# Moving the lead-in of a second feed-forward stage into the last unit of an attention stage, and re-ordering the first group of the first one

## Chip, cores and metric

The kernel runs on one core of one Trainium2 chip. It is one program that is launched once. The metric is its device time in microseconds (us), the median of several runs; the profile is of one further execution. Instruction lines (L1046 and so on) are those of the kernel before; where a line of the changed kernel is meant, the text says so.

## What is computed

The input is x of shape (2, 4096, 256). The reference is a layer of three residual blocks; the first and the third use the same weights:

```python
    x = L0_attn_x
    x = x + 0.5 * _L0_ffn_ref(_layernorm(x, axis=-1), L0_ffn_Wr, L0_ffn_We)
    x = x + _L0_attn_ref(_layernorm(x, axis=-1), L0_attn_Wq, L0_attn_bq, L0_attn_Wk, L0_attn_bk, L0_attn_Wv, L0_attn_bv, L0_attn_Wo, L0_attn_bo)
    x = x + 0.5 * _L0_ffn_ref(_layernorm(x, axis=-1), L0_ffn_Wr, L0_ffn_We)
```

The feed-forward block sends each token to the 2 best of 8 experts (a 256 x 256 matrix each), with a capacity per expert that is counted in the order of the tokens. The attention has 16 heads of 16 features, rotary positions and a softmax over 4096 keys, and ends in an output projection with bias.

## The kernel before

The program is three blocks of code, one after the other; all five engines meet at a barrier between two of them.

**First block (front_phase).** It takes the 8192 tokens in 16 groups of 512: layer norm, routing, experts, and the projections of q, k, v of the groups before. Ahead of the loop each engine does the routing of group 0. TensorE (PE) turns and projects it (`turn`, `router`), waits until the low parts of all weights are made (`pe.wait_ge(s_wl, 2)`), and then does `positions(0)`. VectorE (DVE) makes these low parts, `wel` (L667), `wql` (L671) and `wvl` (L672), and then the choice of experts `pick(0)`. GpSimd (POOL) makes the low part of the activations (`lower`, L765) and the counts (`route`, L786 to L791).

**Attention (attend_phase).** It works on 64 units: 16 pairs of heads times 4 stretches of 1024 queries. A unit has 32 steps over the keys (j = 0 to 31); a step has two halves, and in each half PE does two score products (L1036, 512 columns, operands on 50 of 128 rows), in their shadow two products for the row maxima of the next unit (L1015, on the other rows), and then the products of four earlier exponentials with v (L1046, `times_v`; recorded as 8 rows). ScalarE (ACT) takes the exponential of each score tile (L1114, 128 a unit); DVE takes the maxima (L1139). Three banks hold scores: `score` waits for the exponential three tiles back. The last unit has no maxima to make: `find` returns at once, so DVE has nothing to do in it.

SyncE (SP) runs the transfers in the order of the code. In the last pair of heads it fetches, behind unit 60, what the third block needs first (`fetch`), and behind unit 62 it writes the reciprocals of the softmax sums and reads them back for the first two groups (`fetch_reciprocals`, L1245 and L1248). Ahead of this it must send the output of unit 62 (L964), which ACT copies after tile 8 of unit 63 (`take_output`, L1105).

**Third block (back_phase).** Again 16 groups of 512 tokens. The lead-in of group 0 runs before the loop: bias product (L1429), `spread_out` (L1372, lays the reciprocals over the rows), `normalise_heads` (L1510), `project` (L1379), `add_residual` (L1517), `statistics`, root (ACT, L1464), `newton`, `normalise` (ACT, L1471), `turn` (L1389), `turned` (ACT, L1479 and L1481), `router` (L1398), `pick`, `route`, `positions` (L1405, L1406), and for group 1 everything up to `add_residual`. Then come the expert products of group 0 (L1422) in chunks of 6 matmuls and the weighted sums on DVE (L1559).

## Time and profile before

| | us |
|---|---|
| median of 3 runs (6259.62 to 6266.20) | 6264.52 |
| the profiled execution, its own time | 6264.74 |
| its span in the trace | 6262.9 |

| stretch of the profiled execution | from | to |
|---|---|---|
| first block | 0 | about 670 |
| attention | about 674 | 5757.7 |
| lead-in of the third block | 5757.7 | 5791.4 |
| expert loop of the third block | 5791.4 | 6262.9 |

Busy shares over the span are PE 99%, DVE 94%, ACT 78%, POOL 6%. PE's ends are modelled, so its share says little; the timelines say more. In a timeline a row is a run of like instructions: start, time from the first start to the last end, engine, line, operation, output and inputs, count, and in brackets the idle time ahead of it and what ended it. Granted clock 1.00 is 2.4 GHz, 0.50 is 1.2 GHz.

### The profile page before, as it was taken

How to read it: one execution, taken by the hardware profiler on the slowest of the kernel's cores; microseconds unless marked ns; L12 is line 12 of the kernel's file. 1: busy time of each engine (PE TensorE's matmuls, PEld its weight loads, DVE VectorE, ACT ScalarE, POOL GpSimd, SP SyncE). 2: the span in 40 equal slices, each digit the busy share in tenths (PEclk: the TensorE clock that was granted, in tenths of full speed). 3: DMA queues.
4: the chain of work that ended last, by engine and by line, in shares of the span. 5: the costliest groups of instructions: out<-in, count | busy, mean ns of one | idle time of the engine just before them, and what ended most of it. 6: DMA issues, size and time to landing. Idle time of an engine off the chain costs nothing. (4 is left out here: it accounts for less than half of the span.)

```text
span 6262.9 us, 158275 instructions
## 1 busy us (share of the span) xinstructions
PE 6191.1 (99%) x54276; PEld 2765.9 (44%) x54276; DVE 5907.4 (94%) x6787; ACT 4864.3 (78%) x8953; POOL 398.4 (6%) x604
## 2 busy tenths in 40 slices
PE   8999999999999999999999999999999999999999
PEld 6887333333333333333333333333333333333787
DVE  7998999999999999999999999999999999992777
ACT  4443488888888888888888888888888888887221
POOL 3443100000000000000000000000000000000222
PEclk9998799999999999999999999999999999999999
DMA  2335010101010101010101010101010101000110
GB/s 84 124 121 145 12 17 14 17 14 17 14 17 14 17 14 17 14 17 14 17 14 17 14 17 14 17 14 17 14 17 14 17 14 17 3 22 23 56 56 31
DMA packets 121413, 175.91 MB, mean 28 GB/s; under 512 B 62016, under 2 KB 78944, under 8 KB 117728
## 3 DMA queue, kind: packets, MB, share of 16 engines
q1 hardware_dynamic: 120928, 168.25, 11.8%
q8 instruction: 451, 7.39, 0.5%
q14 instruction: 34, 0.28, 0.0%
HBM read 98.47 MB, written 69.73 MB: 27 GB/s over the span
## 5 line engine op out<-in xcount | busy, mean ns | idle before, releaser
L1139 DVE TENSOR_REDUCE at_mx<-at_m 128x1 f32<-128x1024 f32 x4028 | 4928.7, 1224 | 49.9 <-PE at_m L1015 29.4
L1114 ACT ACTIVATE at_ex<-at_s 128x512 f32<-128x512 f32 x8192 | 4450.1, 595 | 608.1 <-PE at_s L1036 39.4
L1036 PE MATMUL at_s<-at_q,at_k 50*128 50x512 f32 x8192 | 2997.4, 444 | 0.0
L1015 PE MATMUL at_m<-at_k,at_q 48*128 48x512 f32 x8040 | 2928.9, 443 | 2.7 <-issue 2.7
L1046 PE MATMUL at_po<-at_ex,at_v 128*32 128x256 f32 x32816 | 2625.0, 392 | 0.0
L1015 PEld LDWEIGHTS at_m<-at_k,at_q 48*128 48x128 f32 x8040 | 1185.2, 185 | 1662.7 <-DVE at_mx L1139 1592.9
L1046 PEld LDWEIGHTS at_po<-at_ex,at_v 128*32 128x32 f32 x32816 | 646.4, 108 | 1488.8 <-issue 751.2
L1036 PEld LDWEIGHTS at_s<-at_q,at_k 50*128 50x128 f32 x8192 | 1212.0, 185 | 41.0 <-ACT at_ex L1114 40.6
L986 POOL COPY at_v<-at_vst 128x1024 f32<-128x1024 f32 x16 | 16.6, 1036 | 4457.4 <-DMA at_vst<-v_by_head 4457.2
L1422 PE MATMUL bk_ps<-sh_weh,bk_xl 128*128 128x512 f32 x512 | 169.4, 412 | 6.2 <-DVE bk_acc L1559 6.2
L1464 ACT ACTIVATE bk_root<-bk_var 128x4 f32<-128x4 f32 x16 | 3.3, 205 | 212.8 <-DVE bk_var L1531 212.8
L1422 PE MATMUL bk_ps<-sh_wel,bk_xh 128*128 128x512 f32 x512 | 161.3, 396 | 0.0
L1422 PE MATMUL bk_ps<-sh_weh,bk_xh 128*128 128x512 f32 x512 | 161.3, 396 | 0.0
L1559 DVE SCALAR_TENSOR_TENSOR bk_acb<-bk_ps,bk_weight,bk_acc 128x256 f32<-128x256 f32 x192 | 92.8, 484 | 55.4 <-PE bk_ps L1422 46.4
L1559 DVE SCALAR_TENSOR_TENSOR bk_acc<-bk_ps,bk_weight,bk_acb 128x256 f32<-128x256 f32 x256 | 123.9, 484 | 9.1
L373 PE MATMUL fr_ps<-sh_weh,fr_xl 128*128 128x512 f32 x352 | 115.4, 409 | 5.2 <-DVE fr_acc L598 4.9
L510 ACT ACTIVATE fr_parts<-fr_rot 128x1024 fp32r<-128x1024 f32 x32 | 34.2, 1069 | 105.8 <-DVE fr_rot L653 105.8
L373 PE MATMUL fr_ps<-sh_weh,fr_xh 128*128 128x512 f32 x352 | 111.5, 398 | 0.0
L373 PE MATMUL fr_ps<-sh_wel,fr_xh 128*128 128x512 f32 x352 | 111.2, 397 | 0.0
L1422 PEld LDWEIGHTS bk_ps<-sh_wel,bk_xh 128*128 128x128 f32 x512 | 96.6, 189 | 23.1
L1422 PEld LDWEIGHTS bk_ps<-sh_weh,bk_xh 128*128 128x128 f32 x512 | 96.5, 188 | 23.4
L1422 PEld LDWEIGHTS bk_ps<-sh_weh,bk_xl 128*128 128x128 f32 x512 | 91.4, 189 | 31.9 <-DVE bk_acc L1559 10.7
(195 smaller groups left out, 2913.5 us busy)
## 6 DMA issues: line engine op xcount, KB each, us to landing
at_q<-q_parts SPq DMA_DIRECT2D x96, 256.0 KB, 4.9
at_k<-k_parts SPq DMA_DIRECT2D x96, 256.0 KB, 6.2
q_parts<-fr_parts SPq DMA_DIRECT2D x64, 256.0 KB, 2.2
k_parts<-fr_parts SPq DMA_DIRECT2D x64, 256.0 KB, 2.5
attended<-at_o SPq DMA_DIRECT2D x256, 34.0 KB
fr_x<-in_x SPq DMA_DIRECT2D x16, 512.0 KB, 4.3
after_ffn<-fr_acc SPq DMA_DIRECT2D x16, 512.0 KB, 3.0
v_by_head<-fr_v SPq DMA_DIRECT2D x16, 512.0 KB, 4.4
```

Of the source, the lines that this page charges most:

```text
L373: last = pe.matmul(pe_s[BANK[n]][:, :], (xh, xl)[a][0][u][:, c, i * P:(i + 1) * P], (weh, wel)[b][:, c, EP * k:EP * (k + 1), :].rearrange( ...
L510: ac.activation(pt[:, 0, w, :, :], rot[:, :, :], ACT.Copy).then_inc(s_hi, 1)
L986: gp.tensor_copy(V[p][:, :, :, 0:HD], vst[p][:, :, :, :]).then_inc(s_vh, 1)
L1015: ins = pe.matmul(pm[w][:, h * QB:(h + 1) * QB], Q[p][rows, base + i * P:base + (i + 1) * P], K[p][rows, c * CW + h * QB:c * CW + (h + 1) ...
L1036: pe.matmul(ps[event(t) % NS], K[p][rows, j * P:(j + 1) * P], Q[p][rows, sb_ * QU + g * QB:sb_ * QU + (g + 1) * QB], start=True, stop=True ...
L1046: last = pe.matmul(po[W * t:W * (t + 1), cols], V[p][:, w, j, :], Ex[QUAD * (j % NX) + t][:, cols], start=start and half == 0, stop=stop a ...
L1114: ac.activation(Ex[QUAD * (j % NX) + 2 * g + 1 - half][:, :], ps[event(t) % NS], ACT.Exp)\
L1139: ve.tensor_reduce(out=mx[u][:, i, c:c + 1], in_=first[(k + 2) % len(first)][:, 0:CW] if opens else pm[w][:, :], op=ALU.max, axis=AX.X)\
L1422: last = pe.matmul(pe_s[BANK[n]][:, :], (xh, xl)[a][u][:, c, i * P:(i + 1) * P], (weh, wel)[b][:, c, EP * k:EP * (k + 1), :].rearrange("p ...
L1464: ac.activation(root[:, :], var[:, :], ACT.Sqrt).then_inc(s_root, 1)
L1559: ve.scalar_tensor_tensor(out=dst, in0=pe_s[BANK[i * NP + e // EP]][:, (e % EP) * D:(e % EP + 1) * D], scalar=weight[u][:, i, e:e + 1], in ...
```

## The change

It has four parts.

1. The lead-in of the third block moves into unit 63 of the attention. PE's part is cut in 26 pieces, set between steps of the unit. The rows that ACT handled (normalising, turning) are done by DVE; the root is done by GpSimd as a power of 0.5. Only the exponential of the routing stays on ACT, ahead of its step 29. The banks of the row maxima (`at_m`) serve as room.
2. SP's fetches for groups 2 and 3 move from the third block behind the read of the reciprocals in the attention.
3. ACT's loop over the units is cut at step 10 of a unit in place of its start; the order of the scores is that of all other units (`PAIRED` is KT, so the other order is never taken).
4. In the first block PE does the first two expert chunks ahead of `positions(0)` and waits there for `wel` alone; DVE makes `wql` and `wvl` in group 0, between its chunks 12 and 13.

```diff
@@ first block, PE, ahead of the loop
-                pe.wait_ge(s_wl, 2)
+                pe.wait_ge(s_wl, 1)
+                experts(0, 0, 0, 2)
                 positions(0)
...
@@ first block, DVE, body (taken away: the same three lines ahead of pick(0))
                     if here:
                         combine(g, u, it, 10, 13)
+                    if isinstance(g, int) and g == 0:
+                        ve.wait_ge(s_wh, 2)
+                        ve.tensor_tensor(wql[:, :, :, :], pq_in[:, :, :, :], wqh[:, :, :, :].bitcast(F32), ALU.subtract)
+                        ve.tensor_tensor(wvl[:, :, :], pv_in[:, :, :], wvh[:, :, :].bitcast(F32), ALU.subtract).then_inc(s_wl, 1)
                     if after:
                         pick(g + 1)
...
@@ attention, SP
                         if not more and sb_ == SB - 1:
-                            fetch_reciprocals(sp)
+                            fetch_reciprocals_ahead(sp, ahead, sources, late.s_tick)
+                            for g in range(2):
+                                fetch_group(sp, ahead, late, sources, g + 2, g)
...
@@ attention, PE, last unit
                 pairs(pe, pair)
+                last_unit(0, 2)
+                pe.wait_ge(s_mr, 2 + NPAIR * SB * RED)
+                pe.wait_ge(ahead.s_c, 4 * DMA)
+                for c in range(NC):
+                    last = pe.matmul(pm[0][:, GT:GT + D], ahead.bv[:, c, :], ahead.wo[:, c, :], start=(c == 0), stop=(c == NC - 1))
+                last.then_inc(late.s_bv, 1)
+                last_unit(2, 4)
+                step.spread_out(pe, 0, 0, 0)
+                last_unit(4, 6)
+                pe.wait_ge(late.s_bo, 1)
+                for m in range(TG * NC):
+                    step.project(pe, 0, m, m + 1)
+                    last_unit(6 + m, 7 + m)
+                last_unit(14, 15)
+                step.spread_out(pe, 1, 1, 0)
+                last_unit(15, 18)
+                for c in range(NC):
+                    step.turn(pe, 0, c, c + 1)
+                    last_unit(18 + c, 19 + c)
+                for m in range(2):
+                    step.project(pe, 1, m, m + 1)
+                    last_unit(20 + m, 21 + m)
+                for i in range(TG):
+                    step.router(pe, 0, i, i + 1)
+                    last_unit(22 + i, 23 + i)
+                for m in range(2, TG * NC):
+                    step.project(pe, 1, m, m + 1)
+                    last_unit(24 + m, 25 + m)
+                step.positions(pe, 0)
...
@@ attention, ACT
-                with loop(nc, ac, 0, NPAIR * SB) as u:
-                    unit(u)
+                unit(0, 0, CUT * QUAD)
+                with loop(nc, ac, 0, LAST) as u:
+                    unit(u, CUT * QUAD)
+                    unit(u + 1, 0, CUT * QUAD)
+                unit(LAST, CUT * QUAD, 29 * QUAD)
+                step.exponential(ac, 0)
+                unit(LAST, 29 * QUAD)
...
@@ attention, DVE, behind the maxima
                 invert_sums(ve, ahead, 0)
+                ve.wait_ge(s_s, LAST * TILES + 2)
+                ve.wait_ge(late.s_bv, 1)
+                ve.tensor_tensor(ahead.bo[:, :], ahead.bo[:, :], pm[0][:, GT:GT + D], ALU.add).then_inc(late.s_bo, 1)
+                step.normalise_heads(ve, 0, 0, 0)
+                for j in range(2):
+                    step.add_residual(ve, 0, 0, j)
+                step.statistics(ve, 0, late.y[0])
+                step.newton(ve, 0)
+                step.normalise_here(ve, 0, late.y[0])
+                step.normalise_heads(ve, 1, 1, 0)
+                step.turned_here(ve, 0, 0)
+                step.pick(ve, 0)
+                step.odds(ve, 0)
+                for j in range(2):
+                    step.add_residual(ve, 1, 1, j)
+                step.room(ve, 0)
...
@@ attention, GpSimd, behind its pairs
+                step.biased(gp, 0, 0, 0)
+                step.root_by_power(gp, 0)
+                step.biased(gp, 1, 1, 0)
+                step.lower(gp, 0, 0)
+                step.route(gp, 0, 0)
...
@@ new functions
+def fetch_group(sp, t, late, sources, g, u):
+
+    attended, residual, reciprocals, _, _ = sources
+    hold(sp, late.s_an, g - 1, late.s_tick)
+    for c in range(NC):
+        sp.dma_start(t.at[u][:, c, :], attended(g, c)).then_inc(t.s_at[u], DMA)
+    sp.dma_start(t.rec[u][:, :].bitcast(F32), reciprocals(g)).then_inc(t.s_rec[u], DMA)
+    hold(sp, late.s_xb, g - 1, late.s_tick)
+    sp.dma_start(t.x[u][:, :, :], residual(g)).then_inc(t.s_x[u], DMA)
...
+    def spread_out(pe, n, u, it):
+
+        pe.wait_ge(s_rec[u], it * DMA + DMA)
+        need(pe, s_y, n * 2 - 1)
+        pe.matmul(py[0][:, :], spread[:, :], rec[u][:, :], start=True, stop=True).then_inc(s_pr, 1)
...
+    def root_by_power(gp, n):
+        hold(gp, s_var, n + 1, s_tick)
+        gp.tensor_tensor(root[:, :], var[:, :], r0[:, :], ALU.pow).then_inc(s_root, 1)
+
+    def normalise_here(ve, n, src):
+        ve.wait_ge(s_nw, (n + 1) * NEWTON)
+        for i in range(TG):
+            last = ve.tensor_scalar(xn[:, i, :], src[:, i, :], mv[:, i, 0:1], rs[:, i:i + 1], ALU.subtract, ALU.mult)
+        last.then_inc(s_xn, 1)
+
+    def turned_here(ve, n, u):
+        ve.wait_ge(s_tr, n + 1)
+        for c in range(NC):
+            ve.tensor_copy(xt[:, c, :], pT[c][:, :])
+        for c in range(NC):
+            last = ve.tensor_copy(xh[u][:, c, :], pT[c][:, :])
+        last.then_inc(s_ev, 1)
```

The instructions of PE at the boundary between attention and third block, before. `at_po` is the output of the attention, `bk_py`, `bk_pT` and `bk_pz` are banks of the third block, and "waits" names what the instruction waits for:

```order
L1046 MATMUL at_po<-at_ex,at_v 32x256 x7
L917 UNCONDITIONAL_BRANCH
L1366 UNCONDITIONAL_BRANCH [waits barrier_Pool_Activation_PE_DVE_SP_release]
L1429 MATMUL bk_py<-bk_wo,bk_bv 128x256 [waits bk_const]
L1429 MATMUL bk_py<-bk_wo,bk_bv 128x256
L1372 MATMUL bk_py<-bk_rec,bk_spread 128x512 [waits bk_rec0,bk_recs]
L1379 MATMUL bk_py<-bk_wo,bk_an 128x256 [waits bk_an,bk_bias]
L1379 MATMUL bk_py<-bk_wo,bk_an 128x256 x7
L1389 MATMUL bk_pT<-sh_ident,bk_xn 128x128 [waits bk_xn]
```

The same place now (the lines are those of the changed kernel):

```order
L1438 MATMUL at_m<-bk_chosen,sh_before 128x32 [waits bk_chosen]
L1439 MATMUL at_m<-bk_pre,sh_ones 128x32
L1073 MATMUL at_po<-at_ex,at_v 32x256 [waits at_exp]
L1073 MATMUL at_po<-at_ex,at_v 32x256 x7
L927 UNCONDITIONAL_BRANCH
L1685 UNCONDITIONAL_BRANCH [waits barrier_Pool_Activation_PE_DVE_SP_release]
L1700 MATMUL bk_ps<-sh_weh,bk_xl 128x512 [waits bk_xlow]
L1700 MATMUL bk_ps<-sh_weh,bk_xl 128x512
```

Behind the barrier the expert products come at once; what stood between is ahead of it.

PE in steps 3 to 5 of the last unit, before (`at_s` is a score bank):

```order
L1036 MATMUL at_s<-at_q,at_k 128x512 [waits at_exp] x2
L1046 MATMUL at_po<-at_ex,at_v 32x256 x4
L1036 MATMUL at_s<-at_q,at_k 128x512 [waits at_exp] x2
L1046 MATMUL at_po<-at_ex,at_v 32x256 [waits at_exp]
L1046 MATMUL at_po<-at_ex,at_v 32x256 x3
```

And now, the same steps, with the wait for the reciprocals of group 0 (`bk_rec0`) ahead of step 4:

```order
L1063 MATMUL at_s<-at_q,at_k 128x512 [waits at_exp] x2
L1073 MATMUL at_po<-at_ex,at_v 32x256 x4
L1401 MATMUL at_m<-bk_rec,bk_spread 128x512 [waits bk_rec0]
L1063 MATMUL at_s<-at_q,at_k 128x512 [waits at_exp] x2
L1073 MATMUL at_po<-at_ex,at_v 32x256 [waits at_exp]
L1073 MATMUL at_po<-at_ex,at_v 32x256 x3
```

A product of the lead-in, with a wait of its own, stands in the row of the unit's products.

SP in the last pair, now:

```order
L976 DMA attended<-at_o 17x512 [waits at_mq,at_exp]
L976 DMA attended<-at_o 17x512 x3
L1329 DMA reciprocals<-bk_split 16x512 [waits bk_recs]
L1329 DMA reciprocals<-bk_split 16x512 x15
L1332 DMA bk_rec<-reciprocals 32x512 [waits bk_recout]
L1332 DMA bk_rec<-reciprocals 32x512
L1345 DMA bk_at<-attended 128x512 [waits bk_an]
```

Up to the read of `bk_rec` this order is that of before; the fetch of group 2 behind it is new here.

## Rows read from the trace of the kernel before

**Rows 1.** Timeline of PE at the end of the attention and in the lead-in.

```profile
5754.66 0.73 PE L1036 MATMUL at_s<-at_q,at_k 50*128 50x512 f32 x2
5755.32 2.37 PE L1046 MATMUL at_po<-at_ex,at_v 128*32 128x256 f32 x40
5761.47 1.10 PE L1429 MATMUL bk_py<-bk_wo,bk_bv 128*128 128x256 f32 x4 [3.78 <-PEq L917]
...
5778.00 1.97 PE L1389 MATMUL bk_pT<-sh_ident,bk_xn 128*128 128x128 f32 x8 [7.24 <-ACT bk_xn L1471]
```

**Rows 2.** Chain that ended last, in order of time, same place: start, us, what.

```profile
5785.70 5.68 PE bk_py L1379 x16
5791.43 5.70 PE bk_ps L1422 x24
```

**Rows 3.** Timelines of PE and ACT in the last unit.

```profile
5687.02 0.73 PE L1036 MATMUL at_s<-at_q,at_k 50*128 50x512 f32 x2
...
5700.54 0.73 PE L1036 MATMUL at_s<-at_q,at_k 50*128 50x512 f32 x2
...
5701.08 1.09 ACT L1114 ACTIVATE at_ex<-at_s 128x512 f32<-128x512 f32 x2
```

**Rows 4.** Timelines of PE and ACT in unit 0, at the low clock.

```profile
690.15 0.79 PE L1036 MATMUL at_s<-at_q,at_k 50*128 50x512 f32 x1
...
690.99 1.08 ACT L1114 ACTIVATE at_ex<-at_s 128x512 f32<-128x512 f32 x2 [1.07 <-PE at_s L1036]
...
692.31 0.79 PE L1036 MATMUL at_s<-at_q,at_k 50*128 50x512 f32 x1
```

**Rows 5.** Timeline of SP in the last unit.

```profile
5684.52 8.04 SPq L1245 DMA_DIRECT2D reciprocals<-bk_split  x16
5694.14 0.79 SPq L1248 DMA_DIRECT2D bk_rec<-reciprocals  x2
```

**Rows 6.** The view of line L1248, from issue to landing.

```profile
DMA to landing us min/median/max: 1.9/1.9/1.9
```

**Rows 7.** Chain that ended last, third block; its first row follows an idle PE.

```profile
5820.59 6.01 PE bk_ps L1422 x18
...
5832.34 0.43 PE bk_py L1372
...
5838.57 0.87 PE bk_pT L1389 x8
...
5842.25 1.68 PE bk_pz L1398 x16
5843.94 3.56 PE bk_py L1379 x16
```

**Rows 8.** Stretches: length, busy (count) of PE, PEld, DVE, ACT, POOL, clock, DMA.

```profile
620.00:668.00 48.00, 46.95 (x84) 20.65 (x84) 48.00 (x44) 0.00 (x0) 0.00 (x0) 0.50 0.08 27
688.00:706.00 18.00, 18.00 (x104) 6.07 (x100) 10.12 (x9) 9.28 (x17) 1.97 (x1) 0.50 0.03 7
...
5690.00:5756.00 66.00, 66.00 (x544) 24.33 (x547) 0.00 (x0) 58.33 (x108) 0.00 (x0) 1.00 0.03 7
...
5816.00:5820.00 4.00, 0.46 (x2) 0.03 (x1) 3.93 (x4) 0.23 (x1) 0.43 (x3) 1.00 0.00 0
...
5822.00:5824.00 2.00, 2.00 (x6) 1.58 (x5) 0.96 (x3) 0.00 (x0) 0.00 (x0) 0.50 0.00 0
5824.00:5826.00 2.00, 2.00 (x10) 1.60 (x10) 1.50 (x6) 0.00 (x0) 0.64 (x3) 1.00 0.04 8
```

**Rows 9.** Timelines of PE and DVE in the first group.

```profile
28.50 0.18 PE L356 MATMUL fr_ps2z<-fr_chosen,sh_before 128*128 128x32 bf16 x1 [7.87 <-POOL fr_run L791]
...
19.42 3.37 DVE L671 TENSOR_TENSOR fr_wql<-fr_xn,fr_wqh 128x1024 fp32r<-128x1024 f32 x1
22.72 0.68 DVE L672 TENSOR_TENSOR fr_wvl<-fr_even,fr_wvh 128x512 fp32r<-128x512 f32 x1
...
31.59 0.49 DVE L598 SCALAR_TENSOR_TENSOR fr_acb<-fr_ps,fr_weight,fr_x 128x256 f32<-128x256 f32 x1 [2.65 <-PE fr_ps L373]
```

More of the change, by code:

```diff
@@ L992, in _, with pair @@
                     gp.wait_ge(s_one, 3 + w)
-                def step(r, k, n, more):
+                def pair(r, k, n, more):
                     if more:
@@ L1105, in take_output, with unit @@
                     ac.activation(O[:, :], po[:, :], ACT.Copy).then_inc(s_e, 1)
-                def unit(u):
-                    for t in range(TILES):
+                def unit(u, start=0, end=TILES):
+                    for t in range(start, end):
                         j, half, g = t // QUAD, t % QUAD // 2, t % 2
+                        slot = 2 * half + 1 - g if isinstance(u, int) and u == LAST and j >= PAIRED else 2 * g + 1 - half
                         if t % QUAD == 0:
@@ L1254, in back_phase @@
+def back_phase(nc, name, shared, ahead, late, sources, attended_out, out):
+    _, _, _, sums_of, recs_of = sources
     EP = 2
@@ L1425, in experts @@
                         last.then_inc(s_mm, 1)
-                pe.wait_ge(s_c, 4 * DMA)
-                for c in range(NC):
-                    last = pe.matmul(py[1][:, 0:D], bv[:, c, :], wo[:, c, :], start=(c == 0), stop=(c == NC - 1))
-                last.then_inc(s_bv, 1)
-                pe.wait_ge(s_all, 4)
-                spread_out(0, 0, 0)
-                pe.wait_ge(s_bo, 1)
-                project(0)
-                turn(0)
-                spread_out(1, 1, 0)
-                router(0)
-                project(1)
-                positions(0)
                 def body(g, u, it):
```

560 lines of the change are left out of this document (276 added, 284 removed).

## Prediction, made before the changed kernel had run

> **What bounds the kernel now.** I read the stage borders first, then PE's timeline at the end of the attention. The reader is to see there that PE's last product of the attention ends at 5755.32 + 2.37 = 5757.69, that PE starts again behind the barrier at 5761.47 [rows 1], and that the first expert product comes at 5791.43 [rows 2]. The 29.96 us between are a lead-in in which PE mostly waits; one wait alone is 7.24 us [rows 1]. All of this leaves the place where it stood. The barrier with its 3.78 us stays.
>
> The next question is whether the last unit has room for it. DVE does nothing there for the 66 us that were looked at, and ACT is busy 58.33 of them [rows 8]. But the moved products run on PE. The last unit goes from step 4 at 5687.02 [rows 3] to its last half at 5754.66 [rows 1], 55 halves, so 1.230 us a half. Is that PE's own time or a wait for ACT? The score of 5700.54 has its exponential at 5701.08 [rows 3]: ACT takes a score as soon as it is there, and idles ahead of it. At the low clock the same half takes 692.31 - 690.15 = 2.16 us, with ACT idle for 1.07 of it [rows 4], so there PE surely sets the pace. Cutting these 2.16 us in a part that goes with the clock (0.93 at full clock) and one that doesn't (0.30) gives 1.23 again. I conclude that PE bounds the last unit, and that what is put into it is paid in full.
>
> **The change, part by part.**
>
> (a) Removed: 29.96 us between barrier and first expert product.
>
> (b) The wait at step 4. PE now stands there until the reciprocals of group 0 are read back (`bk_rec0`). SP issues this read at 5694.14 [rows 5]; it lands 1.9 us later [rows 6], at 5696.04. Nothing ahead of it on SP changes: 16 writes take 8.04 us from 5684.52 on [rows 5], behind the output of unit 62, which hangs on the copy behind ACT's tile 8, and that lies ahead of the first inserted piece. PE comes to step 4 at 5687.02 [rows 3], with the bias product ahead of it about 0.9 us later. Behind PE are queued all scores, so ACT stands too. With 0.1 us for the signal and 0.43 us [rows 7] x 2.16/1.23 = 0.76 for the spread product, step 4 begins at 5696.9 and not at 5687.02: +9.9 us, the bias product within it. The bounds are 9.5 (full clock) and 10.5.
>
> (c) The other pieces: group 0 and 1 projected 2 x 3.56, one spread product 0.43, turning 0.87, router 1.68 [rows 7], positions 0.05 (between 5785.70 + 5.68 and 5791.43 [rows 2]): 10.15 us. These rows are runs; now they are 24 short pieces between other shapes. A change of shape costs nothing at best, and at most 0.1 us, a third of the fixed 0.30 of a half with its three groups: 0 to 2.4. I take 0.85, nearer to nothing, since most pieces wait for nothing. +11.0 us. If ACT did bound the unit, these would be free; that is a rival.
>
> (d) The clock. PE is idle for some 8 us at step 4. In the trace an idle PE at 5816 to 5820 is followed by clock 0.50 [rows 8]; so step 4 begins at 1.2 GHz. How long does it stay? In dense expert products it was back within about 3.5 us (18 products from 5820.59, clock 1.00 from 5824 [rows 7, 8]). In the very mix of the attention, unit 0, it was still 0.50 over all of 688 to 706, with PE recorded busy all the time; and in products of maxima alone over 620 to 668 [rows 8]. The nearest row is that of the mix: some 18 us, or 9 halves of 0.93 = 8.4 us, and 0.7 for two or three pieces in them (16 take 5.68 at the low clock [rows 2] against 3.56 [rows 7], 0.27 for a piece of two). +9.1 us. The ends are 1.5 us (dense rows) and the rest of the unit, 56 halves x 0.93 = 52 us and the pieces at 1.8 times their time, 8 us: 60 us.
>
> The Trainium skill, page "TensorE: Matmul & The Clock Gate", section "Part 1: The HAM clock gate (the 'warmup' mystery)", says that the array is slow by default and that sustained activity gives it full clock at the first busy look. By that rule the mix would be back as fast as dense products. The row of unit 0 speaks against it.
>
> (e) The chain behind each piece. PE waited 7.24 us for sum, statistics, root and rows [rows 1]; now five steps, 12.3 us, lie between the last piece of `project(0)` and `turn`. The root on GpSimd and a DVE that copies four tiles of 128 x 512 aren't in the trace; a weighted sum of 128 x 256 takes DVE 0.49 [rows 9], so the copies some 4 us, against three steps (7.4 us) up to the router. From router to the first expert product it was 5.7 us [rows 2]; the exponential now stands 9.8 us behind it. Nothing, then; if the root took over 4 us, PE would stand for the excess. SP's new transfers for groups 2 and 3 stand behind the reciprocals and ahead of the last output, some 25 steps early: nothing. ACT's loop has the same body: nothing.
>
> (f) The first expert products now follow an idle of 3.78 us. Such a start costs 6.01 us for 18 products [rows 7] against 18/24 x 5.70 = 4.28 [rows 2]: +1.7 us (0 to 3).
>
> (g) First group. PE idles 7.87 us ahead of `positions` [rows 9]; two expert chunks fill part of it. `pick` comes up to 3.37 + 0.68 = 4.05 us earlier, and with it the first weighted sum, at 31.59 before [rows 9]. Then DVE does the two subtractions at group 0's end. They took 4.05; by the 0.68 of the smaller one, which has half the elements, the two would take 2.0 where nothing slows them, and a part falls into DVE's idle time. I take 2.0 back: -2.0 us, between -4.05 and 0, for no more is given back than was won.
>
> **Sum.** -29.96 + 9.9 + 11.0 + 9.1 + 1.7 - 2.0 = -0.3 us. The profiled execution took 6264.74 by its own clock, 0.2 above the median of 6264.52. So 6264.
>
> **The rivals.**
>
> 1. The clock is back quickly (18 in 100). For it: pieces are dense full-array products, and in dense rows it took 3.5 us. Against it: unit 0, and the first two steps have no pieces. Then (d) is 1.5: 6264 - 7.6 = 6256.5. The same time follows from the skill's rule above.
> 2. The clock doesn't come back in the last unit (12 in 100). This is the one that ends slower: without maxima the scores use 50 of 128 rows, and products of maxima alone never got the clock back in 48 us [rows 8]. Against it: at full clock the same unit holds it [rows 8], and the pieces add dense work. Then (d) is 60: 6315. It decides from 45 us at the low clock on; if it comes back between 25 and 60 us (9 in 100), 6267 to 6284.
> 3. ACT bounds the unit, the pieces are hidden (8 in 100). For it: ACT is busy 58.33 of 66 us [rows 8]. Against it: exponentials start at the arrival of their scores [rows 3]. Then (c) is 0: 6253, and with a quick clock 6245.
> 4. The wait at step 4 isn't there, since the reciprocals come earlier than rows 5 say (3 in 100): without (d) and without (b) but for 1.3 of pieces, 6246.
>
> **How the numbers follow.** The forecast, a net of nothing, has 50 in 100, with its own range 6255 to 6274. The range for 8 in 10 takes in rivals 1 and 3 but for the latter's end, and the late return of the clock: 6250 to 6288. A measurement of this kernel can tell some 0.2%, 12.5 us, from no change. Faster by more: most of rivals 3 and 4 and a little of 1 and the forecast, 0.13. Slower by more: rival 2, the late half of its neighbour and an unforeseen stall, 0.21. Within: 0.66.
>
> **What would show each step.** In the profile after: PE idle by some 8 us ahead of `spread_out` with the DMA `bk_rec` as releaser (b); granted clock 0.50 behind it, and where it returns (d); halves of 1.23 us without a piece and about 1.70 with one (c), or 1.23 for both (rival 3); the first expert product some 3.8 us behind the last product of the attention (a), the first four microseconds of them slow (f); DVE's first weighted sum at about 27.5 us (g). The prediction is wrong if the clock behaves otherwise than in unit 0, or if a piece costs much more than its row.

## The result and the profile after

The changed kernel takes 6317.88 us (median of 4 runs, 6305.74 to 6323.36) against 6262.07 us before (4 runs beside it, 6259.52 to 6266.20). The ratio is 1.0083, 95% interval 1.0071 to 1.0095: slower by 0.8%; the two medians are 55.8 us apart. The forecast was 6264 us with a range up to 6288. The second of the rivals is what came, "the clock doesn't come back in the last unit", at 6315 us.

The profiled execution took 6322.34 us, its span is 6320.5. The first view to open is the timeline of PE around step 4 of the last unit; it answers to rows 3. Lines are those of the changed kernel: L1063 scores, L1073 weighted values, L1401 the spread product, L1409 a piece of the projection, L1430 one of the router, L1700 expert products. In a row of PE, `50*128 50x512` means that 50 rows and 128 columns of the array hold the fixed operand and 512 columns stream through it. A router piece is two products in the code and stands as x4: the trace has two records for each product of it.

```profile
5688.93 0.73 PE L1063 MATMUL at_s<-at_q,at_k 50*128 50x512 f32 x2
5689.59 0.64 PE L1073 MATMUL at_po<-at_ex,at_v 128*32 128x256 f32 x8
5698.18 0.79 PE L1401 MATMUL at_m<-bk_rec,bk_spread 32*128 32x512 f32 x1 [7.96 <-DMA bk_rec<-reciprocals]
5698.90 1.22 PE L1063 MATMUL at_s<-at_q,at_k 50*128 50x512 f32 x2
...
5707.54 1.22 PE L1409 MATMUL at_m<-bk_wo,bk_an 128*128 128x256 f32 x2
5708.70 1.22 PE L1063 MATMUL at_s<-at_q,at_k 50*128 50x512 f32 x2
...
5713.02 1.22 PE L1409 MATMUL at_m<-bk_wo,bk_an 128*128 128x256 f32 x2
...
5791.01 1.02 PE L1430 MATMUL at_m<-sh_wr,bk_xt 128*128 128x8 f32 x4
5791.96 1.22 PE L1063 MATMUL at_s<-at_q,at_k 50*128 50x512 f32 x2
```

Ahead of the wait a pair of scores takes 0.73 us, behind it 1.22. That is the low clock, and it is still there at 5791.96. The second view is the table of stretches: length, then busy time and count of PE, PEld, DVE, ACT and POOL, then the granted clock, DMA share and GB/s.

```profile
5692.00:5700.00 8.00, 1.82 (x3) 0.78 (x3) 0.92 (x2) 0.27 (x1) 0.00 (x0) 0.55 0.19 48
5700.00:5720.00 20.00, 20.00 (x86) 6.96 (x86) 0.37 (x1) 8.41 (x16) 0.00 (x0) 0.50 0.17 57
...
5780.00:5800.00 20.00, 20.00 (x88) 8.26 (x84) 0.00 (x0) 7.60 (x14) 0.87 (x1) 0.50 0.00 1
...
5830.00:5848.00 18.00, 18.00 (x94) 6.39 (x97) 1.48 (x3) 6.51 (x12) 0.21 (x1) 0.50 0.00 0
...
5856.00:5860.00 4.00, 4.00 (x16) 2.81 (x16) 2.96 (x12) 0.10 (x1) 0.00 (x0) 0.93 0.11 37
```

The clock is 0.50 (1.2 GHz) in every stretch from 5700 to 5848 us, with PE recorded busy all the time, and comes back only among the expert products. It stays low although a piece that uses all rows and columns of the array, 1.16 us of work, stands between the scores every 5.48 us (5707.54, 5713.02). The same unit stood at 1.00 over 66 us before [rows 8]. The third view is PE's timeline at the end of the attention, which answers to rows 1 and 2.

```profile
5845.11 3.64 PE L1073 MATMUL at_po<-at_ex,at_v 128*32 128x256 f32 x32
5851.38 1.19 PE L1700 MATMUL bk_ps<-sh_weh,bk_xl 128*128 128x512 f32 x2 [2.63 <-PEq L927]
...
5856.61 0.63 PE L1700 MATMUL bk_ps<-sh_weh,bk_xl 128*128 128x512 f32 x2
...
5868.46 0.73 PE L1700 MATMUL bk_ps<-sh_weh,bk_xl 128*128 128x512 f32 x2 [0.56 <-DVE bk_acc L1749]
...
5881.50 0.73 PE L1700 MATMUL bk_ps<-sh_weh,bk_xl 128*128 128x512 f32 x2 [2.02 <-DVE bk_acc L1749]
```

The lead-in is gone as meant: only the barrier, 2.63 us without work of PE, lies between the last product of the attention and the first of the experts.

The span grew by 57.6 us, and the timelines of both kernels give all of it:

| part | before | after | us |
|---|---|---|---|
| start of the last unit (ACT's copy in its step 2) | 5682.11 | 5684.46 | +2.35 |
| from there to the first score of step 4 | 4.91 | 14.44 | +9.53 |
| from there to the end of the attention (5757.69, 5848.75) | 70.67 | 149.85 | +79.18 |
| from there to the first expert product (5791.43, 5851.38) | 33.74 | 2.63 | -31.11 |
| from there to the end | 471.47 | 469.12 | -2.35 |

The row of +79.18 is what has to be explained. The forecast had 11.0 + 9.1 there. The first row, +2.35, can't be put down to the change: see (g) below.

### The profile page after: what moved, and what is told of

Read it like the earlier page. It is cut to its first block and busy times, and to the rows that moved or that the text cites. A ratio compares the mean times of both kernels' runs of the same rounds, so it can differ in the third digit from the quotient of the medians.

```text
span 6320.5 us, 158147 instructions
## 1 busy us (share of the span) xinstructions
PE 6253.8 (99%) x54276; PEld 2780.1 (44%) x54276; DVE 5911.3 (94%) x6795; ACT 4856.8 (77%) x8942; POOL 400.1 (6%) x606
## 5 line engine op out<-in xcount | busy, mean ns | idle before, releaser
L1063 PE MATMUL at_s<-at_q,at_k 50*128 50x512 f32 x8192 | 3025.0, 448 | 0.0
L1073 PE MATMUL at_po<-at_ex,at_v 128*32 128x256 f32 x32816 | 2651.6, 395 | 0.0
L1073 PEld LDWEIGHTS at_po<-at_ex,at_v 128*32 128x32 f32 x32816 | 649.1, 108 | 1506.1 <-issue 779.7
L1063 PEld LDWEIGHTS at_s<-at_q,at_k 50*128 50x128 f32 x8192 | 1223.7, 186 | 55.6 <-ACT at_ex L1177 42.9
L1700 PE MATMUL bk_ps<-sh_weh,bk_xl 128*128 128x512 f32 x512 | 169.7, 413 | 7.2 <-DVE bk_acc L1749 4.4
L1700 PE MATMUL bk_ps<-sh_wel,bk_xh 128*128 128x512 f32 x512 | 160.7, 395 | 0.0
L1700 PE MATMUL bk_ps<-sh_weh,bk_xh 128*128 128x512 f32 x512 | 160.6, 395 | 0.0
L1700 PEld LDWEIGHTS bk_ps<-sh_wel,bk_xh 128*128 128x128 f32 x512 | 96.7, 189 | 22.4
L1700 PEld LDWEIGHTS bk_ps<-sh_weh,bk_xh 128*128 128x128 f32 x512 | 96.7, 189 | 22.3
L1700 PEld LDWEIGHTS bk_ps<-sh_weh,bk_xl 128*128 128x128 f32 x512 | 91.1, 189 | 34.9 <-DVE bk_acc L1749 11.8
```

Source lines behind the costliest of these rows:

```text
L1063: pe.matmul(ps[event(t) % NS], K[p][rows, j * P:(j + 1) * P], Q[p][rows, sb_ * QU + g * QB:sb_ * QU + (g + 1) * QB], start=True, stop=True ...
L1073: last = pe.matmul(po[W * t:W * (t + 1), cols], V[p][:, w, j, :], Ex[QUAD * (j % NX) + t][:, cols], start=start and half == 0, stop=stop a ...
L1700: last = pe.matmul(pe_s[BANK[n]][:, :], (xh, xl)[a][u][:, c, i * P:(i + 1) * P], (weh, wel)[b][:, c, EP * k:EP * (k + 1), :].rearrange("p ...
```

## The experiments

The theory after this reading (A): PE's idle time at step 4 takes the clock down, and the last unit's own products can't bring it back. The rivals: the small pieces hold the clock down with or without the wait (B), or they are what keeps it from coming back (C).

**e1, the reciprocals early.** SP stores and fetches them in the last unit but one:

```
-                        if not more and sb_ == SB - 1:
+                        if not more and sb_ == SB - 2:
                             fetch_reciprocals_ahead(sp, ahead, sources, late.s_tick)
+                        if not more and sb_ == SB - 1:
                             for g in range(2):
                                 fetch_group(sp, ahead, late, sources, g + 2, g)
```

> The changed kernel with one thing moved: SyncE stores and fetches the reciprocals of the first two groups during the last unit but one (about 14 us ahead of where they are needed) instead of behind the output of that unit, so that bk_rec0 has landed long before step 4 of the last unit. The pieces stay where they are. Theory A, the 8 us idle of TensorE takes the clock down, and without it the clock stays at 1.00 for the last unit: the profile shows no idle of TensorE at L1401 ahead of step 4, windows of the last unit at 1.00, the unit about 74 us shorter (8 of the wait, about 66 of the low clock, from the changed kernel's 167 us between ScalarE's copy and the first expert product against 82 before + 8 + 11 of pieces), so about 6248 us. Theory B, the small pieces (32- to 256-column float32 products and the change between shapes) hold the clock down with or without the wait: only the 8 us go, the windows stay at 0.50 for more than 100 us, about 6314 us.

Measured: 6249.10 us (6239.07 to 6264.57, 10 runs) against 6264.29 before, ratio 0.9971 (0.9960 to 0.9982). The median is 69 us under that of the changed kernel, as A said and B excludes. But the ten runs fall apart: 6239 to 6242 in four, 6248 to 6265 in six. The profiled one, 6261.25, is of the second kind, and its stretches and PE's timeline (L1064 scores, L1431 router pieces) show why:

```profile
5690.00:5720.00 30.00, 30.00 (x224) 11.45 (x223) 8.59 (x23) 22.24 (x42) 3.79 (x5) 1.00 0.01 2
5734.00:5736.00 2.00, 2.00 (x14) 0.87 (x14) 0.00 (x0) 1.18 (x3) 0.00 (x0) 1.00 0.03 8
5736.00:5738.00 2.00, 2.00 (x15) 1.18 (x14) 0.00 (x0) 0.99 (x2) 0.00 (x0) 0.77 0.00 0
5738.00:5740.00 2.00, 2.00 (x11) 0.70 (x10) 0.00 (x0) 1.09 (x2) 0.00 (x0) 0.50 0.00 0
5740.00:5780.00 40.00, 40.00 (x170) 14.86 (x168) 2.43 (x13) 16.38 (x31) 2.29 (x11) 0.50 0.00 1
```

```profile
5733.61 0.61 PE L1431 MATMUL at_m<-sh_wr,bk_xt 128*128 128x8 f32 x4
5734.15 0.73 PE L1064 MATMUL at_s<-at_q,at_k 50*128 50x512 f32 x2
...
5736.60 0.62 PE L1431 MATMUL at_m<-sh_wr,bk_xt 128*128 128x8 f32 x4
5737.16 1.22 PE L1064 MATMUL at_s<-at_q,at_k 50*128 50x512 f32 x2
```

Step 4 and 50 us behind it run at 1.00, pieces and all. Then the clock falls at 5737.16, right behind the second router piece, with PE never idle, and stays down to the end of the unit. So B is wrong for the whole, and something of it is right at one place.

**e2, the wait alone.** The kernel before, with one line added at step 4 of the last unit, and no piece:

```
+                            if isinstance(u, int) and u == NPAIR * SB - 1 and j == 4 and half == 0:
+                                pe.wait_ge(ahead.s_rec[0], DMA)
```

> The kernel before, with one wait added and nothing else: TensorE waits at step 4 of the last unit for the landing of bk_rec0. No piece is moved. Theory A with its second half, that the last unit's own products (scores and weighted values, no maxima) can't bring the clock back: windows at 0.50 from about 5700 us to the end of the unit, 28 steps at about 2.16 us over the 2.1 they take at the full clock (+60 us) and 8 us of wait, so about 6330 us. Rival C, that it is the pieces between the steps which keep the clock from returning: the clock is back within some 20 us as in unit 0, and the kernel takes 8 + about 9 more than before, about 6280 us.

Measured: 6330.50 us (6322.85 to 6337.03, 4 runs), ratio 1.0102 (1.0083 to 1.0121). One wait on PE costs 66 us. PE's timeline and the stretch behind the wait:

```profile
5687.93 0.64 PE L1046 MATMUL at_po<-at_ex,at_v 128*32 128x256 f32 x8
5697.36 1.22 PE L1036 MATMUL at_s<-at_q,at_k 50*128 50x512 f32 x2 [8.79 <-DMA bk_rec<-reciprocals]
...
5825.51 2.05 PE L1431 MATMUL bk_py<-bk_wo,bk_bv 128*128 128x256 f32 x4 [4.03 <-PEq L917]
```

```profile
5700.00:5815.00 115.00, 115.00 (x532) 37.12 (x531) 0.00 (x0) 57.67 (x107) 0.00 (x0) 0.50 0.00 1
```

0.50 for 115 us and more, without a single piece. From step 4 to the end of the attention (5825.51 - 4.03 = 5821.48) it is 124.12 us, where before it was 70.67: the low clock alone costs 53.4 us, on top of the wait's 8.8. C falls; both halves of A hold.

**e8, the wait and a run of full-array products behind it.** What does the unit lack to bring the clock back? The kernel e2 with 16 products of 128 rows and 256 columns behind the wait:

```
+                                pe.wait_ge(ahead.s_c, 4 * DMA)
+                                pe.wait_ge(s_mr, 2 + NPAIR * SB * RED)
                                 pe.wait_ge(ahead.s_rec[0], DMA)
+                                for n in range(16):
+                                    pe.matmul(pm[n % 2][:, 0:D], ahead.wo[:, 0, 0:P], ahead.wo[:, 1, :], start=True, stop=True)
```

> e2_wait_only (the kernel before with the 8.8 us wait at step 4 of the last unit) and directly behind the wait 16 products of 128 rows and 256 columns in float32 (wo by wo, into the two buffers of the maxima, which nobody reads any more), about 0.85 us each at the low clock and about 0.4 at the full. e2_wait_only stayed at 0.50 from 5697 us to the end of the unit, 6330.5 us. Theory A': what the unit lacks to bring the clock back is products that fill all rows and columns; the burst brings it back within 5 to 9 us and the rest of the unit runs at 1.00: 6330 - 60 + 8, about 6278 us. Rival: once down, the clock stays down for the unit whatever is in between, or falls again at once: about 6330 + 13 = 6343 us.

Measured: 6281.79 us (6277.14 to 6287.48, 7 runs), ratio 1.0030 (1.0019 to 1.0041). 49 us less than e2, though 9.85 us of useless work were added. The two waits ahead are for the weights and the free banks that these products need; the row names the read of the reciprocals as the last to come. PE's timeline (here L1063 is the added product, 16 of them recorded as 32) and the stretches:

```profile
5688.45 9.92 PE L1063 MATMUL at_m<-bk_wo 128*128 128x256 f32 x32 [8.81 <-DMA bk_rec<-reciprocals]
5698.30 0.73 PE L1036 MATMUL at_s<-at_q,at_k 50*128 50x512 f32 x2
```

```profile
5692.00:5694.00 2.00, 2.00 (x6) 1.62 (x5) 0.00 (x0) 0.00 (x0) 0.00 (x0) 0.50 0.00 0
5694.00:5696.00 2.00, 2.00 (x10) 1.72 (x10) 0.00 (x0) 0.00 (x0) 0.00 (x0) 0.98 0.00 0
5700.00:5760.00 60.00, 60.00 (x491) 22.01 (x490) 0.00 (x0) 52.98 (x98) 0.00 (x0) 1.00 0.00 1
```

The clock is back 5.6 us after the burst began (5688.45 to about 5694), and the very unit that couldn't raise it then holds it for 60 us. From its first score behind the burst to the end of the attention it takes 70.68 us, as before. Raising and holding are two things.

**e3 and e4, the first group.** Both put the first group back to the order of before (VectorE's two subtractions ahead of the first `pick`, no expert chunk ahead of `positions`); e3 is otherwise the changed kernel, e4 is e1.

```
-                pe.wait_ge(s_wl, 1)
-                experts(0, 0, 0, 2)
+                pe.wait_ge(s_wl, 2)
                 positions(0)
...
```

> The changed kernel with the first group as in the kernel before (subtractions of the projection's low parts ahead of the first pick, no experts ahead of positions); the last unit as in the changed kernel. What the trace suggests: the changed order wins 5.1 us at the first expert product (23.4 for 28.55 us), loses 2.1 by two waits for bk-style sums and 2.6 + low clock at 54.1 us behind the subtractions that VectorE now does ahead of group 1's pick, and stands 1.9 to 2.4 us behind at the last unit; so this kernel should have ScalarE's copy of the last unit at about 5682.1 instead of 5684.5 us and take about 2 us less, about 6316 us. Rival: the 2.35 us come from elsewhere (chance of the first block's transfers), and the copy stands at 5684.5 here too.

> Both of the former: reciprocals fetched early and the first group as before. Theory A and additive parts: about 6246 us, 2 us under e1_rec_early and 16 under the kernel before; first expert product of the second network at about 5776 us. Theory B: about 6312 us.

Measured: e3 6323.89 us (4 runs, ratio 1.0094, 1.0077 to 1.0111), e4 6244.68 us (6240.01 to 6269.42, 10 runs, ratio 0.9977, 0.9963 to 0.9991). e3's ratio and that of the changed kernel (1.0083, 1.0071 to 1.0095) overlap, so the times can't tell 2 us here. ACT's copy in the last unit is at 5677.53 in e3, neither at the 5682.1 that was expected nor at the rival's 5684.5. In e4 seven runs lie at 6240 to 6245 and three at 6262 to 6269. Its profiled execution is one of the seven, and it is where the pieces can be priced at the full clock (L1058 scores, L1404 projection, L1425 router):

```profile
5685.06 0.50 PE L1396 MATMUL at_m<-bk_rec,bk_spread 32*128 32x512 f32 x1
5685.48 0.73 PE L1058 MATMUL at_s<-at_q,at_k 50*128 50x512 f32 x2
...
5690.40 0.70 PE L1404 MATMUL at_m<-bk_wo,bk_an 128*128 128x256 f32 x2
5691.03 0.73 PE L1058 MATMUL at_s<-at_q,at_k 50*128 50x512 f32 x2
...
5737.63 0.61 PE L1425 MATMUL at_m<-sh_wr,bk_xt 128*128 128x8 f32 x4
5738.17 0.73 PE L1058 MATMUL at_s<-at_q,at_k 50*128 50x512 f32 x2
...
5773.57 0.70 PE L1695 MATMUL bk_ps<-sh_weh,bk_xl 128*128 128x512 f32 x2 [2.62 <-PEq L921]
```

A projection piece moves the next score by 0.63 us, a router piece by 0.54. From the first score of step 4 to the end of the attention (5770.95) it is 85.47 us, 14.80 more than before. The mean of e4's ten runs, on which its ratio rests, is less far below before than the median, because of the three.

**e5, e6, e7, the router pieces.** Theory D says that a stretch whose only pieces are narrow (8 columns) can take the clock; E says that it falls by chance anywhere. E has some support in the kernel before: in the four series that stand beside the experiments, 3 to 5 of its 17 to 30 runs are above 6270 us, at a mean granted clock of 0.986 to 0.988 against 0.988 to 0.991 in the others, with none of the moved work. No trace of such a run exists. e5 puts each router piece beside a projection piece, e6 puts all four in one lump, e7 issues each twice. The base of all is e4. The edit of e5:

```
                 for i in range(TG):
                     step.router(pe, 0, i, i + 1)
+                    step.project(pe, 1, 2 + i, 3 + i)
                     last_unit(22 + i, 23 + i)
-                for m in range(2, TG * NC):
+                last_unit(26, 30)
+                for m in range(6, TG * NC):
                     step.project(pe, 1, m, m + 1)
                     last_unit(24 + m, 25 + m)
```

The edit of e6:

```
-                for i in range(TG):
-                    step.router(pe, 0, i, i + 1)
-                    last_unit(22 + i, 23 + i)
+                step.router(pe, 0)
+                last_unit(22, 26)
```

The edit of e7:

```
                 for i in range(TG):
+                    need(pe, late.s_ev, 1)
+                    for c in range(NC):
+                        pe.matmul(pm[1][:, (TG + i) * E:(TG + i + 1) * E], late.xt[:, c, i * P:(i + 1) * P], shared[1][:, c, :],
+                                  start=(c == 0), stop=(c == NC - 1))
                     step.router(pe, 0, i, i + 1)
```

> e4_both (reciprocals early, first group as before) with the same pieces in another order: each of the four router pieces (four products of 8 columns, 0.61 us) stands in one step with a projection piece of the second group (256 columns, 0.70 us) instead of in a step of its own; steps 26 to 29 have no piece. Three of ten executions of e4_both took 6262 to 6269 us and the other seven 6240 to 6245; in the profiled execution of e1_rec_early the granted clock fell to 0.50 at 5737.2 us, right behind the second router piece, with no idle of TensorE. Theory D, it is the stretch of steps with nothing but narrow pieces that takes the clock: with wide products beside them nearly all executions are at 6240 to 6245 us, mean clock 0.991 or more, median about 6242. Rival E, the last unit's own mix loses the clock by chance wherever the pieces stand: about three in ten still at 6262 to 6269 us.

> e4_both with all four router pieces in one lump of 16 products (about 2.2 us) ahead of step 22, steps 23 to 25 without a piece. Theory D: the stretch with narrow products alone is shorter over all (one lump and three plain steps), yet the densest narrow stretch is longer; if the narrow products themselves take the clock it falls in at least as many executions as in e4_both (3 in 10), at this one place. Rival E: as e4_both, 3 in 10 by chance, median about 6244 us. If what counts is the alternation of narrow pieces with score steps over some 12 us, it falls in fewer, median about 6242.

> e4_both with the suspected cost doubled: each router piece is issued twice (the first time into columns that nobody reads; its values are not used). Adds 4 x about 0.5 = 2 us at the full clock. Theory D: the clock falls in nearly every execution, at about the router pieces, median about 6265 us with mean clock 0.987 to 0.988. Rival E: 2 us on top of e4_both, median about 6247 us, three in ten with a fallen clock.

Measured, with the runs of each in us:

| kernel | median | ratio to before | runs |
|---|---|---|---|
| e4 | 6244.68 | 0.9977 (0.9963 to 0.9991) | 7 at 6240 to 6245, 3 at 6262 to 6269 |
| e5 | 6255.10 | 0.9989 (0.9980 to 0.9998) | 9 at 6249 to 6258, 2 at 6264 and 6265 |
| e6 | 6268.43 | 1.0006 (0.9996 to 1.0015) | all 10 at 6260 to 6279 |
| e7 | 6265.64 | 0.9999 (0.9987 to 1.0011) | 3 at 6244 to 6246, 7 at 6259 to 6276 |

The same work in one lump leaves all ten runs at 6260 and above, where spread over four steps three were. That the clock fell at the lump is seen in the one trace, and for the other nine runs it is read from their times and mean clocks (0.985 to 0.988). The stretches of e6 show the place; the lump is at 5739.35:

```profile
5739.00:5741.00 2.00, 2.00 (x23) 1.66 (x15) 0.00 (x0) 0.74 (x2) 0.00 (x0) 1.00 0.03 8
5741.00:5743.00 2.00, 2.00 (x14) 0.78 (x13) 1.43 (x8) 1.09 (x2) 0.00 (x0) 0.70 0.00 0
5743.00:5750.00 7.00, 7.00 (x31) 2.52 (x32) 0.66 (x4) 3.26 (x6) 1.40 (x7) 0.50 0.00 0
```

D is borne out by e6. e7 points the same way, seven of ten against three of ten, but so few runs can't part the two, and its traced execution kept the clock. e5 missed its number, 6255 for 6242. Its traced execution kept the clock through all router pieces, the last of which ended at about 5748, and lost it some 10 us later, at a place that I hadn't looked at:

```profile
5755.38 0.64 PE L1068 MATMUL at_po<-at_ex,at_v 128*32 128x256 f32 x8
5757.17 0.99 PE L1058 MATMUL at_s<-at_q,at_k 50*128 50x512 f32 x2 [1.16 <-ACT at_ex L1174]
...
5758.97 1.22 PE L1058 MATMUL at_s<-at_q,at_k 50*128 50x512 f32 x2
```

```profile
5756.52 2.56 ACT L1174 ACTIVATE at_ex<-at_s 128x512 f32<-128x512 f32 x5 [1.85 <-issue]
```

PE waits 1.16 us for ACT, and ACT had stood 1.85 us for nothing the trace shows ("issue"). A gap like it is in e4 (1.72 us, which the trace puts down to a score of PE), where projection pieces around it left PE a wait of 0.40 us only. e5's two runs at 6264 and 6265 have no trace; rival E had expected some of that kind.

**e9 and e10, cover.** The projection pieces are laid so that steps 26 to 28 have one too. e9 has the first group of before, e10 the changed one.

```
-                for m in range(2):
-                    step.project(pe, 1, m, m + 1)
-                    last_unit(20 + m, 21 + m)
+                step.project(pe, 1, 0, 1)
+                last_unit(20, 22)
                 for i in range(TG):
                     step.router(pe, 0, i, i + 1)
+                    step.project(pe, 1, 1 + i, 2 + i)
                     last_unit(22 + i, 23 + i)
-                for m in range(2, TG * NC):
+                for m in range(5, TG * NC):
                     step.project(pe, 1, m, m + 1)
-                    last_unit(24 + m, 25 + m)
+                    last_unit(21 + m, 22 + m)
+                last_unit(29, KT)
```

> e5_router_beside with the pieces without a router partner moved: projection pieces of the second group at steps 20, 22 to 25 (beside the router pieces) and 26, 27, 28; steps 21, 29, 30 and 31 have none. In e5_router_beside the clock fell at 5757.2 us in the profiled execution and in most others (9 of 11 at 6252 us or more where a kept clock gives 6240 to 6245), behind steps 26 to 29 without a piece and a wait of 1.16 us for ScalarE's exponential, which itself had stood 1.85 us for no releaser at one place of its straight-line code; in e4_both, with pieces there, the same standstill made TensorE wait only 0.40 us and the clock stayed. Theory D with its second half (narrow pieces, and a wait of a us where the steps have no wide products, each can take the clock): both causes are gone, nearly all executions at 6240 to 6246 us, median 6243, mean clock 0.991 or more. Rival E, chance falls wherever the pieces stand: 3 in 10 at 6255 to 6269 us.

> e9_cover with the first group in the changed kernel's order (first expert pieces ahead of the positions, the projection's low parts subtracted later). If the first group's new order wins what was forecast: 2 us less than e9_cover, about 6241 us median, all executions within 5 us. If it loses what the one profiled execution seemed to show (last unit 2.35 us later than before): 6245 us.

Measured: e9 6246.60 us (6239.91 to 6254.70, 9 runs, ratio 0.9974, 0.9964 to 0.9984), e10 6246.15 us (6239.75 to 6256.06, 9 runs, ratio 0.9973, 0.9964 to 0.9983). No run is above 6256.1 any more; none of 18 is in the group at 6260 and above, which had three of e4's ten. But in each kernel four of nine runs are at 6250 to 6256. PE still waits 0.66 us (e9) and 0.60 us (e10) for ACT there. The two medians are 1.5 to 1.9 us above e4's.

**e11, ACT back in its loop.** e10, with the 88 straight-line exponentials of the last unit back in the loop, and the router's exponential behind them; DVE's `add_residual` of group 1 also moves ahead of `odds`:

```
-                unit(0, 0, CUT * QUAD)
-                with loop(nc, ac, 0, LAST) as u:
-                    unit(u, CUT * QUAD)
-                    unit(u + 1, 0, CUT * QUAD)
-                unit(LAST, CUT * QUAD, 29 * QUAD)
+                with loop(nc, ac, 0, NPAIR * SB) as u:
+                    unit(u)
                 step.exponential(ac, 0)
-                unit(LAST, 29 * QUAD)
...
-                step.odds(ve, 0)
                 for j in range(2):
                     step.add_residual(ve, 1, 1, j)
+                step.odds(ve, 0)
```

> e10_cover_new_group with ScalarE's part of the last unit put back into its loop (no straight-line code of 88 exponentials), the router's exponential of group 0 behind the unit's last exponential instead of at step 29, and VectorE's add_residual of group 1 ahead of odds. In the profiled executions with the straight-line code ScalarE stood 1.7 to 2.0 us with no releaser at about 5754 us and TensorE then waited 0.40 to 1.16 us; four of nine executions of e9_cover and of e10_cover_new_group took 6250 to 6256 instead of 6240 to 6246 us. Theory F, that this small wait still takes the clock in those executions: the standstill and TensorE's wait are gone, all executions at 6238 to 6245, median about 6241 us. Rival: the spread comes from elsewhere (unit 0, the first block), the 6250 to 6256 stay in about four of ten, median 6246, or the later exponential holds up the first weighted sum of the second network by 1 to 2 us.

Measured: 6243.36 us (6239.83 to 6247.33, 5 runs) against 6262.50 before, ratio 0.9964 (0.9951 to 0.9977). PE has no wait in the whole unit, and the stretches stand at 1.00:

```profile
5680.00:5720.00 40.00, 40.00 (x298) 15.13 (x297) 8.38 (x23) 30.11 (x57) 5.95 (x9) 1.00 0.10 32
5720.00:5760.00 40.00, 40.00 (x305) 16.77 (x301) 7.36 (x20) 28.28 (x53) 3.78 (x8) 1.00 0.09 29
```

None of five runs is above 6248, against eight of eighteen in e9 and e10. That fits F, but doesn't show it: five runs are few, no trace of a run at 6250 to 6256 exists, and the rival that the spread comes from elsewhere stands. e12 below has neither the pieces nor the straight-line code, and its runs spread nearly as far, 6254 to 6267 us; unit 0 makes such a spread, see (g). The later exponential cost the first expert product 1.13 us (its wait is 3.75 us for 2.62), and the clock is at 0.50 behind this longer wait (5774 to 5776), so that from there to the end e11 takes 468.24 us for e10's 466.85.

**e12, the first group alone** in the kernel before; the edit is e3's with plus and minus exchanged.

> The kernel before with the changed order of the first group and nothing else. As forecast: 2 us less than before, 6262 for 6264 us. First expert product at about 23 us for 28.5; the transposes that stand at 45.5 us before at about 43. Rival: the 2.6 us wait at 54 us and the low clock behind it eat the gain, no difference or up to 2 us slower.

Measured: 6262.23 us (12 runs) against 6262.50, ratio 0.9995 (0.9986 to 1.0003): too small for the times. The traces can price it at an early mark, the transposes at about 105 us. In the nine traces with the old order (before, e2 to e9) they start at 105.47, 108.63, 108.27, 105.79, 108.85, 108.69, 108.17, 105.81 and 107.24 us, in the five with the new one (after, e1, e10, e11, e12) at 107.83, 103.91, 106.45, 105.17 and 103.86. The means are 107.4 and 105.4: 2.0 us gained, less than the spread within either group.

## Why the prediction was wrong, by its steps

**(d), the clock, is the step that failed.** It took 9.1 us "by the nearest row", unit 0, "the very mix of the attention". Unit 0 isn't the mix of the last unit. Every step of unit 0 also has products of maxima for the unit to come, and the last unit has none; I had written that difference down myself in the second rival, and gave it 12 in 100. Unit 0's clock came back at 690 to 709 us, depending on the trace, so the 18 us weren't a bad reading of unit 0. Scores and weighted values alone left it at 0.50 for the rest of the unit in e2. That it's the missing products of maxima which make this difference is argued and not shown: no kernel had them behind such a wait. The upper end that I had worked out and set aside was near: its 52 us for the halves are 53.4 in e2, and its 60 with the pieces are 79.18 - 14.80 = 64.4 in the changed kernel, at e4's price for the pieces. By the medians e8 saves more, 48.7 us and the burst's 9.85, 58.6 in all; what is beyond 53.4 lies outside this stretch, and where the last unit begins differs by 8.9 us between the two traces alone, see (g). The idle of 4 us at 5816 [rows 8] was rightly read: an idle PE takes the clock down. The rows of dense products [rows 7, 8] were too: e8 needed some 5.6 us. What neither row said is whether *this* work can raise the clock. The range should have had the full remaining time in it, and even 60 us would have put its end at 6315, 3 us short: (c) was too small as well.

The Trainium skill, "TensorE: Matmul & The Clock Gate", section "Part 1: The HAM clock gate (the 'warmup' mystery)", was rightly set aside as a forecast: by its rule sustained activity releases the throttle at the first busy look, and here 150 us of work with PE recorded busy didn't, where e8's unbroken run of products on the full array did. The second half of what that page says, in "HAM oscillation — how this bites in real kernels", that a wait for a DMA between bursts is what throttles PE, agrees with e2 against before (1.00 and 0.50 in the last unit).

**(b), the wait at step 4,** was right: +9.9 forecast, +9.53 measured, and its parts too (7.96 us of idle, the read issued at 5696.30 and landed 1.8 to 2.1 us later). The whole stands 2 us later than forecast, since the unit began later.

**(c), the pieces,** was undersized. 11.0 us were forecast from step 4 on, 14.80 measured at the full clock (e4). A projection piece costs 0.63 and not 3.56 / 8 = 0.445 (16 x 0.185 = 3.0 us), a router piece 0.54 and not 0.42 (0.5), and 0.40 is the wait for ACT. These come on top of the 10.15 of the rows and make 14.1; a turning piece, 0.58 for 0.435, adds 0.3, and 0.4 isn't placed. The bound for a change of shape, "at most 0.1 us", was too low: it is 0.12 to 0.19 for these pieces. At the low clock a projection piece is 1.16 us (5707.54 to 5708.70), a router piece 0.95. So (c) and (d) together at their upper end gave 71 us and measured 79.2. Rival 3, hidden pieces, is excluded by the same rows.

**(a)** was right (33.74 of before became 2.63; the barrier alone is 1.15 shorter). **(e)** was right in all kernels: PE waits for nothing of the chain. The root on GpSimd takes 1.03 us and the four copies on DVE 2.57 (the bound was 4). What wasn't seen is ACT's standstill in its new straight-line code, under "same body: nothing". **(f)** the slow first products are there, from 5851.38 to about 5856.6, but not by the cause that I gave. The clock was already low ahead of the barrier. In e4, e7, e9 and e10, which kept it in the last unit, it stays at 1.00 over the barrier's 2.6 us without work, and e4's first pair takes 0.70 us; in e11, with 3.75 us, it fell. And I left out what follows: before, PE waited 4.12 us for DVE at 5820.59 and started at the low clock again [rows 7], and now it waits 0.56 and 2.02 and keeps the clock. Net -2.35 with the slow start in it, -4.94 without it (e4).

**(g), the first group,** forecast -2.0, and the marks say -2.0; with traces that differ by 3 to 4 us within either order, that close a match is luck. The first expert product is at 23.42 for 28.55 us, DVE's first weighted sum at 29.51 for 31.59 (forecast 27.5), and part is given back, as said, but by another road: the two subtractions now stand ahead of group 1's `pick` and PE waits 2.59 us at 54.09 and is at 0.50 behind it. Rows of DVE's and PE's timelines, and the stretch:

```profile
47.89 1.98 DVE L746 TENSOR_TENSOR fr_wql<-fr_xn,fr_wqh 128x1024 fp32r<-128x1024 f32 x1
49.79 0.68 DVE L747 TENSOR_TENSOR fr_wvl<-fr_even,fr_wvh 128x512 fp32r<-128x512 f32 x1
...
54.09 1.22 PE L373 MATMUL fr_ps<-sh_weh,fr_xl 128*128 128x512 f32 x2 [2.59 <-DVE fr_acc L603]
```

```profile
54.00:56.00 2.00, 1.92 (x5) 1.53 (x6) 1.00 (x3) 0.00 (x0) 0.81 (x4) 0.50 0.00 0
```

The +2.35 at the start of the last unit in the table above is not (g). That start lies anywhere from 5674.65 (e8) to 5684.46 us (after) in the fourteen kernels' traces, whichever first group they have. Unit 0 makes much of this. Its clock comes back at about 707.4 us in the trace of before, 709.3 in that of after and 690.2 in that of e8, though the code up to there is the same in before and e8 (the first stretch is of before, the second of e8):

```profile
706.00:708.00 2.00, 2.00 (x16) 0.50 (x12) 1.22 (x1) 1.11 (x3) 0.00 (x0) 0.64 1.62 205
```

```profile
690.00:692.00 2.00, 2.00 (x24) 0.86 (x24) 1.48 (x2) 1.29 (x3) 0.00 (x0) 0.96 0.00 0
```

A us at 0.50 there costs 0.93 / 2.16 = 0.43 us by the prediction's split of a half, so an estimate of 17.3 x 0.43 = 7.4 us between before and e8; their last units begin 7.46 us apart. A difference of a few us between the traces of two kernels ahead of the last unit therefore says nothing about the change.

**The sum, with the wait away:** for e4 the trace gives -31.12 (lead-in) + 1.22 (bias product, spread) + 14.80 (pieces) - 4.94 (behind the first expert product) = -20.0 us, without what lies ahead of the last unit, and the median of e4 is 19.6 below that of before. The forecast's own terms for this kernel are -29.96 + 1.3 + 11.0 + 1.7 = -16.0. They come near partly by luck: the pieces cost 3.8 more, and behind the first expert product it is 4.9 won for 1.7 lost. The change's idea was sound. One wait, 8 us long, turned -19.6 (e4) into +59.6 (e3, the same kernel but for the wait), by medians.

## What to carry to other kernels

Before a wait is put on TensorE, ask two things of the trace: will the wait take the clock, and can the work behind it raise it again? Look for a stretch with exactly that work behind an idle PE, and if there is none, keep the full remaining time at the low clock in the range. If the wait can't go, products on all rows and columns in one run behind it can pay (e8: 9.85 us spent, 53.4 saved); if it can, move the transfer that it waits for (e1: two lines, 69 us). Small products cost more between other shapes than in a run of their own. Products of few columns are best spread out (e4 against e6, 24 us by medians); setting them beside others of 256 columns took the runs at 6260 and above away in e9 and e10, and the median didn't get better.

## What the runs showed of the hardware that I had not expected

- A mix of products can hold the granted clock at 1.00 for 60 us (before, e8) and not raise it from 0.50 in 110 us (e2, 5700 to 5815) with PE recorded busy in both.
- The clock can fall with PE never recorded idle: behind 16 recorded products of 8 columns in one lump (e6's trace; all its ten runs took 6260 us or more), and behind twice four of them between scores (e1's trace). e4's three runs at 6262 to 6269 have no trace.
- In unit 0 the clock comes back anywhere from 690 to 709 us in the same work (fourteen traces).
- PE idle for 2.6 us at the barrier kept the clock at 1.00 (e4, e7, e9, e10), and 3.75 us took it (e11).
- A wait of 1.16 us between steps without pieces was followed by the low clock (e5); with 0.40 to 0.69 us in e4, e7, e9 and e10 the traced runs kept it.
- ACT stood 1.85 to 2.01 us with no releaser at one place of straight-line code of 88 exponentials (e5, e7, e9, e10), and not where they ran in the loop (e11). Its cause wasn't tried.
